# Cross-attention with a two-expert mixture layer: expert outputs scattered onto the residual rows, and every gathered row transposed on TensorE

## The reference, cut to what matters

```python
x = x + attention(ctx, ctx, layernorm(x), Wk, Wv, bv, Wq, bq, Wo, bo)
xn = layernorm(x)
probs = softmax(xn @ w_router)                 # T x 16
top_k_probs, ei = top_k(probs, 2)
# pos = place of each (k, row) in its expert, all first choices ahead of all second ones
buf[ei, pos] = xn, where pos < cap              # cap = 512; later ones are dropped
h = silu(buf @ w_gate) * (buf @ w_fc)          # 512 -> 256, per expert
o = h @ w_proj                                 # 256 -> 512, per expert
y = sum_k top_k_probs[k] * o[ei[k], pos[k]]    # an index past the end reads the last row (511)
x = x + y
```

## Time and profile before

| | |
|---|---|
| three timed runs | 1663.11, 1666.4, 1667.3 us; median 1666.4 |
| profiled execution | 1664.51 us, its span 1662.8 us |
| TensorE busy | 1506.0 us, 91% |
| VectorE, ScalarE, GpSimd busy | 825.0, 414.2, 305.6 us |
| mean granted TensorE clock | 0.955 |
| attention ends, experts begin | about 1277 us |
| last expert output leaves ScalarE | 1561.6 us |

### The profile page before, as it was taken

How to read it: one execution, slowest core, us unless ns; L and a number is a source line. 1 busy time by engine, 2 the same in 40 slices (tenths; PEclk the granted TensorE clock), 3 DMA queues, 4 the chain that set the end, 5 groups by cost and what they waited for, 6 DMA issues and landing times. The chain is left out here.

```text
span 1662.8 us, 23122 instructions
## 1 busy us (share of the span) xinstructions
PE 1506.0 (91%) x7647; PEld 703.6 (42%) x7647; DVE 825.0 (50%) x2286; ACT 414.2 (25%) x484; POOL 305.6 (18%) x413
## 2 busy tenths in 40 slices
PE   7999799999999999999999999999993999999500
PEld 3444344444444444444444444444441444444200
DVE  4433245555555555555555555555543565555254
ACT  2332221321132123112311231123110344444200
POOL 1000001111111111111111111111112423221276
PEclk9999899999999999999999999999996899999855
DMA  6541245435543554355435543544351999998587
GB/s 186 124 102 38 64 83 119 91 77 103 117 90 77 105 115 90 77 107 113 90 77 108 112 90 78 110 110 90 71 117 41 250 288 292 300 276 253 171 280 256
DMA packets 408830, 221.97 MB, mean 133 GB/s; under 512 B 341720, under 2 KB 358110, under 8 KB 408800
## 3 DMA queue, kind: packets, MB, share of 16 engines
q1 hardware_dynamic: 395040, 186.98, 47.0%
q0 software_dynamic: 12544, 34.34, 7.3%
q10 hardware_dynamic: 1216, 0.28, 0.1%
HBM read 95.46 MB, written 42.73 MB: 83 GB/s over the span
## 5 line engine op out<-in xcount | busy, mean ns | idle before, releaser
L43 PE MATMUL sc<-kT,qt 128*128 128x512 f16 (+1 forms) x896 | 317.0, 359 | 9.5 <-PEq L181 4.9
L44 PE MATMUL sc<-kT,qt 128*128 128x512 f16 (+1 forms) x896 | 316.5, 359 | 0.0
L45 PE MATMUL sc<-kT,qt 128*128 128x512 f16 (+1 forms) x896 | 314.9, 359 | 0.0
L45 PE MATMUL acc<-vv,pT 128*128 128x512 f16 x775 | 293.6, 379 | 0.0
L44 PE MATMUL acc<-vv,pT 128*128 128x512 f16 x775 | 293.6, 379 | 0.0
L43 PE MATMUL acc<-vv,pT 128*128 128x512 f16 x775 | 293.5, 379 | 0.0
L807 DVE TENSOR_SCALAR_CACHE_REDUCE s_sb<-sc 128x512 f32<-128x512 f32 (+1 forms) x224 | 141.2, 630 | 195.2 <-PE sc L45 195.2
L761 ACT ACTIVATE row<-xs 128x512 f16<-128x512 f32 x32 | 20.2, 630 | 572.6 <-DVE xs L858 572.6
L829 DVE TENSOR_TENSOR p_hl<-p_sb,p_hl 128x3200 f16<-128x3200 f32 (+2 forms) x33 | 111.8, 3390 | 55.9 <-ACT p_hl L755 55.9
L43 PEld LDWEIGHTS sc<-kT,qt 128*128 128x128 f16 x896 | 88.0, 98 | 109.2 <-issue 19.2
L45 PEld LDWEIGHTS sc<-kT,qt 128*128 128x128 f16 x896 | 88.1, 98 | 92.1 <-issue 2.7
(11 more groups left out here) (214 smaller groups left out, 2017.1 us busy)
## 6 DMA issues: line engine op xcount, KB each, us to landing
eo_dram<-o_sb SPq DMA_DIRECT2D x64, 256.0 KB
xq<-in_x_dram SPq DMA_DIRECT2D x32, 256.0 KB, 2.7
x_in<-in_x_dram SPq DMA_DIRECT2D x32, 256.0 KB, 3.0
raw_g<-in_L_ffn_w_gate_dram SPq DMA_DIRECT2D x16, 512.0 KB
raw_f<-in_L_ffn_w_fc_dram SPq DMA_DIRECT2D x16, 512.0 KB
raw_p<-in_L_ffn_w_proj_dram SPq DMA_DIRECT2D x16, 512.0 KB, 7.4
x_dram<-x SPq DMA_DIRECT2D x32, 256.0 KB, 3.0
rows_dram<-row SPq DMA_DIRECT2D x32, 256.0 KB, 2.2
```

The source lines that it names most:

```text
L43: pe.matmul(out, s_hi, m_hi, start=first, stop=False)
L44: pe.matmul(out, s_hi, m_lo, start=False, stop=False)
L45: return pe.matmul(out, s_lo, m_hi, start=False, stop=last)
```

## The change

- `eo_dram` and `x1_dram` go. One tensor `y_dram` holds the 4096 residual rows, 512 rows for padding and 16 rows for the last row of each expert; the last two kinds are zeroed in `setup`.
- The routing table gets the probability beside the row number. The probabilities are computed in `place`, per tile.
- GpSimd scatters each output tile, already multiplied by the probability in ScalarE's evacuation, with an add in the DMA onto the rows of `y_dram`. An expert's first scatter waits for all scatters of the expert before.
- Where several rows share an expert's last row, its output goes unweighted to its row of the 16. At the end these 16 rows are multiplied by a 4096 x 16 matrix of weights on TensorE (fp32) and added by VectorE.
- At the end SyncE loads all residual rows (16 DMAs of 512 KB), and ScalarE's queue stores them.
- All row tiles are transposed on TensorE: 0 and 1 before the first two `down` products, 2 and 3 between them and the last two.
- In `setup` four semaphores become one, which counts 64, and the zeroing takes 7 DMAs instead of 8.

```diff
-                    dve.wait_ge(s_bv, 16)
+                    dve.wait_ge(s_small, 64)
...
+                for h in range(CAP // P):
+                    pool.dma_start(y_dram[T + h * P:T + (h + 1) * P, :].rearrange("p (k c) -> p k c", c=P),
+                                   zrow).then_inc(s_zero, 16)
...
+                    act.activation(e_two[:], m12[:, 1:2], ACT.Exp, bias=negm[:]).then_inc(rx_done, 1)
...
                 def place(t):
+                    p_1, p_2 = (P12[:, bass.ds(t, 1), k:k + 1].rearrange("p a k -> p (a k)") for k in range(2))
+                    dve.wait_ge(rx_done, t + 1)
+                    dve.reciprocal(p_1, s_exp[:])
+                    dve.drain()
+                    dve.tensor_tensor(p_2, e_two[:], p_1, ALU.mult)
...
-                def store(e, j):
-                    sp.wait_ge(o_ev, J * e + j + 1)
-                    sp.dma_start(eo_dram[bass.ds(CAP * e + P * j, P), :], o_sb[:, j, :]).then_inc(o_out[j], 16)
-                def transpose_rows(b):
-                    sp.dma_start_transpose(xT[:, b, 2:4].rearrange("p j h k c -> p (j h k) c"),
-                                           rows[:, b, 2 * D * 2:2 * D * 4]).then_inc(xt_dma[b], 16)
...
+                step(E // 2 - 1, 0, False, True)
                 for j in range(J):
+                    sp.wait_ge(o_out[j], 16 * E)
+                sp.dma_start(last_o[:], y_dram[Y_LAST:Y_LAST + E, :]).then_inc(last_in, 16)
+                for n in range(NY):
+                    sp.dma_start(y_sb[:, PER * n:PER * (n + 1), :],
+                                 y_dram[PER * P * n:PER * P * (n + 1), :].rearrange("(n p) d -> p n d", p=P)).then_inc(y_in[n], 16)
...
-                def collect(n):
-                    wait_for(pool, c_use, n - SETS + 1)
...
+                def scatter(e):
+                    for j in range(J):
+                        wait_for(pool, o_out[j], 16 * e)
+                    for j in range(J):
+                        pool.wait_ge(o_ev, J * e + j + 1)
+                        pool.indirect_dma_start(y_dram, bass.IndirectOffsetOnAxis(ap=sidx[:, e, j:j + 1], axis=0),
+                                                o_sb[:, j, :], None, bounds_check=Y_LAST + E - 1, oob_is_err=True,
+                                                compute_op=ALU.add).then_inc(o_out[j], 16)
                 pool.wait_ge(grow_rdy, 1)
+                for e in range(3):
+                    gather(e)
+                pool.wait_ge(sidx_rdy, 1)
                 for e in range(E):
+                    if e + 3 < E:
+                        gather(e + 3)
+                    scatter(e)
...
-                    act.activation(o_sb[:, j, :], po[j % 2][:], ACT.Copy, scale=1.0 / (H_S * W_S)).then_inc(o_ev, 1)
+                    act.activation(o_sb[:, j, :], po[j % 2][:], ACT.Copy, scale=p_now[:, b, j:j + 1]).then_inc(o_ev, 1)
...
+                for n in range(NY):
+                    act.wait_ge(y_add, PER * (n + 1))
+                    act.dma_start(out_t[PER * n:PER * (n + 1)].rearrange("n p d -> p n d"),
+                                  y_sb[:, PER * n:PER * (n + 1), :]).then_inc(y_out, 16)
...
                     if more:
                         rows_T(e + 1, 1, 1 - b)
                     p_low(e, b)
+                    if more:
+                        rows_T(e + 1, 3, 1 - b)
...
+                for t in range(NT):
+                    if t % PER == 0:
+                        dve.wait_ge(y_in[t // PER], 16)
+                    dve.wait_ge(ov_pe, t + 1)
+                    dve.tensor_tensor(y_sb[:, t, :], y_sb[:, t, :], pg[t % 4][:], ALU.add).then_inc(y_add, 1)
...
+                    for half in range(2):
+                        for j in range(2 * half, 2 * half + 2):
+                            if more:
+                                rows_T(2 * m + b + 1, m + b, j, 1 - b)
+                        for j in range(2 * half, 2 * half + 2):
+                            if before:
+                                down(2 * m + b - 1, j, 1 - b)
...
+                for t in range(NT):
+                    wait_for(pe, y_add, t - 3)
+                    pe.matmul(pg[t % 4][:], wT[:, t, :], last_o[:], start=True, stop=True).then_inc(ov_pe, 1)
```

More of the change, by code:

```diff
@@ L99, in build @@
         id_rdy = sem("id_rdy")
+        seen = sem("seen")
         with ExitStack() as attn:
@@ L1151, in experts @@
         o_out = [sem(f"o_out{i}") for i in range(J)]
-        c_in = [sem(f"c_in{i}") for i in range(SETS)]
-        c_use = sem("c_use")
+        last_in = sem("last_in")
+        y_in = [sem(f"y_in{i}") for i in range(NY)]
+        ov_pe = sem("ov_pe")
+        y_add = sem("y_add")
         y_out = sem("y_out")
@@ L1172, in _, with step @@
                       .then_inc(tbl_in, 16)
-                def load_x1(first):
-                    sp.dma_start(x1s[:, bass.ds(first, XT), :],
-                                 x1_dram[bass.ds(first, XT)].rearrange("n p d -> p n d")).then_inc(x1_in, 16)
-                def transpose_rows(b):
-                    sp.dma_start_transpose(xT[:, b, 2:4].rearrange("p j h k c -> p (j h k) c"),
-                                           rows[:, b, 2 * D * 2:2 * D * 4]).then_inc(xt_dma[b], 16)
-                def step(m, b, before, more_gf, more_p):
+                def step(m, b, more_gf, more_p):
                     e = 2 * m + b
-                    if more_p:
+                    if more_gf:
                         wait_for(sp, u_pe, 4 * e)
[L1187 to L1191, removed]
                         sp.wait_ge(wgl, 2 * (e + 2))
                         load_gf(e + 2)
-                    if before:
-                        for j in range(J):
-                            store(e - 1, j)
                     if more_p:
@@ L1357, in _, with table @@
                 gf_low(0, 0)
+                dve.drain()
+                dve.tensor_tensor(is_l[:], rr[:], t1m[:].unsqueeze(2).to_broadcast([P, E, J]), ALU.is_equal)
                 dve.wait_ge(tbl_pe, 1)
-                lower = pg[0][:, 0:E * J].rearrange("p (e j) -> p e j", j=J)
-                dve.tensor_copy(up_t[:], pg[0][:, E * J:2 * E * J])
+                def table(lower, up, out):
+                    dve.tensor_copy(up[:], lower[:, E * J:2 * E * J])
+                    dve.drain()
+                    low = lower[:, 0:E * J].rearrange("p (e j) -> p e j", j=J)
+                    dve.tensor_tensor(grow[:], up[:].rearrange("p (e j) -> p e j", j=J), low, ALU.subtract)
+                    dve.drain()
+                    dve.tensor_tensor(grow[:], cmp[:], grow[:], ALU.mult)
+                    dve.drain()
+                    dve.tensor_tensor(out[:], grow[:], low, ALU.add)
@@ L1361, in _ @@
+                table(pg[0], up_t, g_tok)
                 dve.drain()
-                dve.tensor_tensor(grow[:], up_t[:].rearrange("p (e j) -> p e j", j=J), lower, ALU.subtract)
+                dve.tensor_copy(gidx[:], g_tok[:]).then_inc(grow_rdy, 1)
+                table(pg[1], up_p, g_p)
+                dve.tensor_scalar(s_row[:], rr[:], float(Y_PAD), None, ALU.add)
                 dve.drain()
-                dve.tensor_tensor(cmp[:], cmp[:], grow[:], ALU.mult)
+                dve.tensor_tensor(s_row[:], s_row[:], g_tok[:], ALU.subtract)
@@ L1365, in _ @@
+                dve.tensor_scalar(cmp[:], g_p[:], 0.0, None, ALU.is_le)
                 dve.drain()
-                dve.tensor_tensor(gidx[:], cmp[:], lower, ALU.add).then_inc(grow_rdy, 1)
+                dve.tensor_tensor(s_row[:], s_row[:], cmp[:], ALU.mult)
+                dve.drain()
+                dve.tensor_tensor(s_row[:], s_row[:], g_tok[:], ALU.add)
+                dve.drain()
+                dve.tensor_tensor(e_row[:], e_row[:], s_row[:], ALU.subtract)
+                dve.tensor_scalar(cmp[:], g_p[:], -1.0, 1.0, ALU.mult, ALU.add)
@@ new lines, in _ @@
+                dve.drain()
+                dve.tensor_tensor(e_row[:], e_row[:], is_l[:], ALU.mult)
+                dve.tensor_tensor(cmp[:], cmp[:], is_l[:], ALU.mult)
+                dve.drain()
+                dve.tensor_tensor(s_row[:], s_row[:], e_row[:], ALU.add)
+                dve.tensor_tensor(g_p[:], g_p[:], cmp[:], ALU.add)
+                dve.drain()
+                dve.tensor_copy(sidx[:], s_row[:]).then_inc(sidx_rdy, 1)
+                dve.tensor_scalar(g_p[:], g_p[:], 1.0 / (H_S * W_S), None, ALU.mult)
@@ L1390, in step @@
+                dve.tensor_tensor(w_ov[:], w_ov[:], w_two[:], ALU.add).then_inc(wov_rdy, 1)
                 def step(e, b, more):
@@ L1501, in _ @@
                     down(E - 1, j, 1)
+                pe.wait_ge(wov_rdy, 1)
+                for i in range(NT // 4):
+                    wait_for(pe, wt_sb, i - 3)
+                    for q in range(4):
+                        last = pe.transpose(pg[i % 4][0:E, q * P:(q + 1) * P], w_ov[:, 4 * i + q, :], ident[:])
+                    last.then_inc(wt_pe, 1)
+                pe.wait_ge(wt_sb, NT // 4)
```

(4 more changed lines are left out.)

288 lines of the change are left out of this document (125 added, 163 removed).

## The result

The changed kernel takes 1658.7 us (median of 6 runs, 1657.2 to 1661.6) against 1666.7 (6 runs, 1663.1 to 1667.3) of the kernel before: a ratio of 0.9959, with a 95% interval of 0.9946 to 0.9973. That is 7.9 us less; 1650 us was forecast, 15.2 less by the sum. The profiled execution of after is the slowest of its six (1661.6, span 1659.9), so I read from it the durations and not the last few microseconds of the whole.

What follows compares the result with a forecast made beforehand. TensorE was taken to bound the kernel up to the last expert, then GpSimd's gathers. Terms of -32.7, +12.5, +1.8, +1.7 and +1.5 gave -15.2 us, from 1664.5 to 1649.3, stated as 1650 us, range 1640 to 1658.

Steps and rivals of the forecast that it cites:

- the sum: Whole kernel: the terms -32.7, +12.5, +1.8, +1.7 and +1.5 us add to -15.2 us.
- the closing stage: After the last evacuation: 101.2 us replaced by 10.5 of scatter wait and 58 of loads, product and stores, -32.7 us.
- The wait for the scatters: Closing stage: two landings of 5.0 us in series, scatters issued every 1.30; last landing 10.5 us after the last evacuation.
- Closing product: End of kernel: 32 fp32 matmuls take 56 us at the lower clock, about the pace of the DMA's 53.
- Rival C: Closing stage: loads and stores overlap fully, TensorE at full clock, 33 us instead of 58, time 1625; 9 in 100.
- Rival A: Accumulating scatters land past 10.6 us and hold output tiles, ScalarE and TensorE; 1682 us at 12 us landing; 13 in 100.
- where I had worked out 4.3: Scatter landing by the skill's double count of bytes: 4.3 us instead of 5.0, which would make the time 1648.
- The transposes: Expert stage: 16 more TensorE instructions in each of 14 steady steps, 0.89 us each step, +12.5 us; expert distance 17.3.
- Expert 0: Expert 0's step: a weight pass and block 3's copy on VectorE delay the next expert's matmuls, +1.8 us, at least 0.6.
- Between attention and experts: Behind the last tile: probabilities no longer hidden, +0.9 us, two more table transposes and a cast, +0.8; together +1.7 us.
- Setup: Start of kernel: one shared semaphore delays TensorE's tail transposition, +1.0, more zeroing, 0.5; +1.5 us, between 0 and 4.
- The signs that I named: Forecast wrong if expert distance exceeds 18 us or closing stage is under 60 or over 75; expected 68 to 69.

Runs made afterwards that it cites:

- the first four experiments: The changed kernel with closing product padded to 128 rows, 1641.3 us; with TensorE kept busy ahead of it, 1654.4; without closing product, 1641.5; with plain scatters, 1646.7.
- the five experiments that have the same order of copies and the transposes on TensorE: The first four experiments, and the kernel with the 128-row closing product and separate semaphores for the four setup loads, 1642.1 us.
- experiments 1 to 4 and 6: The first four experiments, and the kernel with the 128-row closing product and blocks 2 and 3 transposed by DMA again, 1647.4 us.
- the last experiment: The 128-row kernel with separate setup semaphores, and expert 0's copies of blocks 2 and 3 put ahead of its weight passes: 1639.1 us.
- the two before it: The 128-row kernel with blocks 2 and 3 transposed by DMA again, 1647.4 us; the 128-row kernel with separate setup semaphores, 1642.1 us.

## Why the prediction was half wrong

Two terms of the closing stage failed, and with them the forecast of 1650 us (and its range, which ended at 1658). The wait for the scatters was taken as 11.0 us and is 16.2. The rest was bounded by the DMA at 317 GB/s, with TensorE hidden, and took TensorE's 55 us at the lower clock, while the DMA needs 46 for all of it. The expert stage with the transposes came out within about 1 us. The first expert matmul is 3.1 us later than forecast in the profiled execution of after, and 1.8 to 3.4 us earlier than forecast in the first four experiments.

**Closing product: the clock was right, the bound wrong.** I counted 56 us for 32 matmuls at the lower level, "about the pace of the DMA", and took 58 for the stage, 57.5 of them from the first load on; measured 54.96 and 60.4. The reason given for the low clock, that TensorE works for only half of the time, is wrong: it works all of it, and the clock stays at 0.50 all the same. And the DMA's pace was not 57. "53 us at 317 GB/s" fell: loads and stores move 406 GB/s at a share of 1.05, and alone take 46. Rival C had named it (loads and stores overlap, TensorE at full clock), but at 33 us, which fell too. From the first load on the stage is 2.9 us over the forecast and 14 over what the bytes need. That it came so near is luck: the DMA's part was 11 us too long (57.5 for 46), and TensorE's, which I took to be covered by it, happened to be of the same size.

**The wait for the scatters: mis-sized, 16.2 us for 10.5 + 0.5.** The mechanism held: expert 15's first scatter waits for all of expert 14's. But the landing is 5.9, not 5.0 (1.8 us for two), and I took the issue of a gather, 1.30, where 1.84 is measured: the two rounds of four lag by 1.8 and 1.6. Together these are the 5.2 us. That an adding transfer also costs GpSimd more was no term of the sum, though the landing had bounds on both sides. Rival A (over 10.6) didn't come.

The Trainium skill ("Collectives: The Full Stack", section "The bandwidth ceiling: the fold count and why AG ≠ RS ≠ AR") counts an adding DMA's bytes twice. The direction agrees; the size is above it: three times the engine time by the estimate above, and a landing of 5.9 where I had worked out 4.3.

**The transposes: right.** The distance is 17.33, TensorE is busy for 160.00 of 160, +12.5. What I missed is that the two halves of the change belong together: without the scatters the transposes on TensorE cost 14.8 us (9.8 to 17.3); with them, and the product over 128 rows, they save 5 to 6 by the medians, for the DMA share of 0.90 becomes 1.09 to 1.20 with DMA transposes, and TensorE then stalls for them twice.

**Expert 0: right within a microsecond.** Forecast +1.8; the step is 15.2 before, 16.6 in after, and 16.3 to 18.0 in the five experiments that have the same order of copies and the transposes on TensorE (16.3, 17.4, 17.6, 17.8, 18.0), +1.1 to +2.8. Where it is short, the next step is longer: from the first expert matmul to expert 14's last evacuation these six take 14.5 to 15.4 us more than before (15.4 in after), where 1.8 + 12.5 = 14.3 were forecast.

**Between attention and experts: about right.** From ScalarE's exponential to the placement, before (the exponential starts at 1270.04) and after:

```profile
1270.33 0.19 DVE L898 TENSOR_TENSOR sel<-ps_m,oh 128x32 f32<-128x32 f32 x1 [0.19 <-PE ps_m L1053]
```

```profile
1272.35 0.31 ACT L774 ACTIVATE rex<-lg,negm 128x16 f32<-128x16 f32 x1 [4.74 <-DVE oh L884]
...
1272.97 0.16 DVE L907 RECIPROCAL P<-s_exp 128x1 f32<-128x1 f32 x1 [0.58 <-ACT e_two L776]
...
1273.31 0.19 DVE L912 TENSOR_TENSOR sel<-ps_m,oh 128x32 f32<-128x32 f32 x1
```

0.96 us instead of 0.29, 0.7 added where 0.9 was forecast. From the last tile's placement product on TensorE to the first expert matmul it is 24.5 us before and 25.5 to 26.0 in the first four experiments, 1.1 to 1.5 more for the 1.7 forecast; in after it is 28.5 (see "The sum").

**Setup: forecast +1.5, not seen.** The placement product of the last tile but one starts at 1256.44 before. In the kernels with the changed setup it starts at 1258.62 (after), 1254.58, 1256.48, 1256.33, 1256.29 and 1257.64 (experiments 1 to 4 and 6), and with separate semaphores at 1255.93 and 1254.63. Single executions thus differ by 4 us here, to both sides of before, and the runs with separate semaphores are no faster. The 2.2 us of after are within that spread.

**The sum.** The closing stage is 5.2 + 2.9 = 8.1 us over the forecast, about the size of the 8.7 between 1650 and 1658.7. In the profiled execution 12.3 us are missing. Of these 8.1 are the closing stage and 1.1 the expert stage (15.4 for 14.3). The other 3.1 come before the first expert matmul, which is 6.3 us later than before, where 3.2 were forecast (-0.2 to +1.4 in the first four experiments). They are the last tile's placement, 2.3 us later than before where 1.5 were forecast for the setup, and a wait between TensorE's transposes for expert 0 and their copy. The profiled execution of the last experiment has the same wait, in the second block:

```profile
1296.48 1.03 PE L1476 MATMUL tp<-ident,rows 128*128 128x128 f16 x8 [0.49 <-DMA rows<-rows_dram,gidx]
...
1300.00 0.69 DVE L1340 COPY xTe<-tp 128x1024 f16<-128x1024 f16 x1 [4.70 <-remote]
```

```profile
1295.85 0.69 DVE L1348 COPY xTe<-tp 128x1024 f16<-128x1024 f16 x1 [4.55 <-remote]
```

In after TensorE was done at 1297.5 and VectorE starts 2.5 us later; GpSimd is released late at about the same moment. In the last experiment it is 2.5 us as well, in the two before it about 1, in the others next to nothing. The cause stays open. So do some 2 us in the middle run of after: the kernel that only keeps TensorE busy ahead of the product saves 2.0 in the closing stage (58.4 from its first load, at 1594.2, to the end), and its one time, 1654.4, is 4.4 lower.

**The signs that I named.** The closing stage was to be wrong if over 75 us: from the last evacuation as it would end if nothing held it, it is 76.6 (72.4 from where it does end). The scatters' issue (1.54 for 1.0) and landing, the DMA rate (406 and then 198 GB/s for 310) and the first expert matmul missed too; the expert distance of 17.3 held.

## What to carry to other kernels

When a stage's limit is taken away, compare what remains by resource with a measured row for each, and ask of the small one what its shape does to the clock: here padding a product over 16 rows with zeros to 128 was worth 14 us of the closing stage, for two memsets. Price an operation that no row shows on every engine that it touches, its issue as well as its landing. And judge coupled edits together: moving transposes off the DMA is a loss alone, and beside scatters that add it was a gain by the medians.

## What the runs showed of the hardware

- An fp32 product over 16 contracted rows, back to back for 55 us, stays at 1.2 GHz (0.50), and one that starts at 1.00 (1596.2) is at 0.50 from 1599 on; over 128 rows (112 of them zeros), same columns, it starts at 0.50, reaches 1.00 and takes 31.6 us in records instead of 54.9, though it then waits for VectorE.
- Loads and stores of 512 KB side by side move 406 to 408 GB/s at a share of 1.05; loads alone had 334 in the stretch from 4 to 14 us of the kernel before.
- An indirect scatter with addition holds GpSimd for 1.54 us (plain 0.97), lands after 5.9 at the end of the kernel (plain 2.8) and takes, as an estimate, about three times the DMA engines' time.
- Beside scatters that add, at a DMA share of 1.09 to 1.20, a DMA transpose of two row blocks takes up to 18.8 us to land, 14.1 at most before.
